# A transformer block on eight cores: the order of layer norm, key and value sums, and query filler

## The chip, the cores and the metric

One Trainium2 chip, eight cores, one launch. Each core writes its own rows of the output. The metric is the device time in microseconds of the slowest core. TensorE multiplies, VectorE (DVE) and ScalarE (ACT) take results out of PSUM and do the element work, GpSimd (POOL) masks and issues the DMAs of weights, SyncE (SP) issues the other loads.

## The reference, cut to what matters

```python
q = (x @ Wq).reshape(B, T, H, Dh)      # x already normalised; 4 x 4096 x 2048, 16 heads
k = (x @ Wk).reshape(B, T, H, Dh)
v = (x @ Wv).reshape(B, T, H, Dh)
scores = jnp.einsum('bthd,bshd->bhts', q, k)
scores = scores * jnp.tril(jnp.ones((T, T)))      # masked scores are 0, not minus infinity
attn = jax.nn.softmax(scores / T ** 0.5, axis=-1)
out = jnp.einsum('bhts,bshd->bthd', attn, v).reshape(B, T, H * Dh)
return out @ Wo
...
x = x + _layernorm(attention(_layernorm(x)))
x = x + _layernorm(ffn(_layernorm(x)))            # ffn: silu(g * gs) * (u * us), then down, 5632 wide
```

Since a masked score is 0, every masked key still counts with weight exp(0) = 1. For a query tile, all key tiles behind it contribute the plain sum of their rows of V.

## The kernel before

Two cores share one batch of 4096 rows, in 32 tiles of 128. The **even core** (side 0) owns tiles 0 to 17, the **odd core** (side 1) tiles 18 to 31. Keys and values are needed for all tiles up to the last own one: 18 on the even core, 32 on the odd one. The even core's other 14 tiles (`sd.tail`) are never keys; only the sum of their normalised rows is used.

**Phase A** (`phase_a`). Work is recorded in program order for each engine, with semaphores between; nothing is reordered afterwards. `stats(t)` loads a tile of x and takes its mean and variance (DVE, then Ln and Exp on ACT), `apply(t)` normalises it (DVE, into `xn`), `turn(t, hf)` transposes half of it on TensorE and copies it out on ACT. `ln_steps` hands out such steps between the projection tiles. `proj_unit` computes V or K for a chunk of up to four tiles and one group g of 512 columns (four heads), with the weights in `wres[0]` (V) or `wres[1]` (K). A tile is 16 matmuls of 512 columns; ACT and DVE copy the tiles out by turns into `stg`, and a unit is stored to DRAM. The program order is V and K of group 0 chunk by chunk, then V1, K1, V2, K2, V3, K3.

`vsum` adds the rows of each V tile: one matmul of the staged tile with a 64-column window of `ebig`, which has ones in columns 31 and 63, so that the sum of tile u lands in rows u and 32+u of bank 6. `vsum_out(g)` copies these sums to `vs`. On the even core it also adds the tail: `tail_sum` needs all 14 tail tiles summed in `xsum` on DVE, splits that sum in two bf16 parts, turns it by 32 matmuls of one column into `sbig`, and 32 matmuls `ps<-wres,sbig` bring it through the weights of V. In group 0 this stands right behind V0.

**Phase B** (`phase_b`) runs heads one after the other, and in a head blocks of up to four query tiles. A step s is 1024 columns of scores: `qk(s)` on TensorE, `exp(s)` on ACT (with a causal mask on POOL), two steps later `pv(s - 2)`, and sums of the weights on DVE (`zacc`) or TensorE (`zmm`). `pv` of a block's first step begins with the product of `ind` and `vs` (the skipped tiles' sums), and waits for `mul` of the block two before, which frees its bank. Projection Q of the next head is filler: single matmuls that a credit rule puts behind the work of a step, from step `q_from` of a head on. The even core has 25 steps in a head. Phase W is the output projection with its layer norms, phase C the ffn.

The helpers record everything, so the trace shows `mm` as L326, transposes as L331, DVE copies as L348, DVE tensor_tensor as L349, ACT copies as L359 and ACT activations as L360.

Of the kernel before, what the change touches and what calls it, by code (L numbers as in the profile page):

```python
# [7 lines left out]
BF16 = mybir.dt.bfloat16  # L8
# [18 lines left out]
class Side:  # L27

    def __init__(self, k):  # L30
        self.k = k
        if k == 0:
            self.own = list(range(NA))
            self.order = list(range(NT))
            self.blocks = [(4, 4), (8, 4), (12, 4), (16, 2), (0, 4)]
            self.npe = {4: 1, 8: 2, 12: 2, 16: 2, 0: 0}

            self.lag = {4: 2, 8: 2, 12: 1, 16: 0, 0: 2}
            self.ffn = [4, 4, 4, 3, 3]
            self.npt = 6  # L40
            self.q_from = 12
        else:
            self.own = list(range(NA, NT))
            self.order = self.own + list(range(NA))
            self.blocks = [(18, 4), (22, 4), (26, 4), (30, 2)]
            self.npe = {18: 2, 22: 3, 26: 3, 30: 2}
            self.lag = {18: 3, 22: 3, 26: 3, 30: 3}
            self.ffn = [4, 4, 3, 3]
            self.npt = 7

            self.q_from = 30
        self.keys = list(range(self.own[-1] + 1))
# [65 lines left out]
def build_nc():  # L118
# [43 lines left out]
    sh.onesb = small("onesb", [128, 128], BF16)  # L162
    sh.ebig = small("ebig", [128, 96], BF16)
    sh.c64 = small("c64", [64, 128], BF16)
# [235 lines left out]
def phase_a(c):  # L400
# [102 lines left out]
    pend = []  # L503

    def flush_vsum():
        while pend:
            pend.pop(0)()

    def proj_tile(kind, g, cc, i, slot, who):
# [23 lines left out]
        if kind == "k":  # L533
            ev = evac(c, who, c.stg[slot][:, i * W:(i + 1) * W], bank(c, pb)[:, 0:W], w)
        else:
            sv = c.stg[slot][:, 0:4 * W].rearrange("p (h t) -> p h t", h=4)[:, :, i * 128:(i + 1) * 128]
            ev = evac(c, who, sv, bank(c, pb).rearrange("p (h t) -> p h t", h=4), w)
            u = gt + i
            first = cc == 0 and i == 0
            fin = cc == len(sd.chunks) - 1 and i == nt - 1 and not sd.tail  # L540

            def vsum(u=u, sv=sv, ev=ev, slot=slot, first=first, fin=fin):
                w = [ev, ev_const] + ([c.ev_vs] if first else [])
                ev_vsmm[slot] = mm(c, bank(c, 6)[0:64, :], c.ebig[:, 31 - u:95 - u], sv, start=first,
                                   stop=fin, waits=w, inc=True)
            pend.append(vsum)
        ev_pb[pb] = ev
        return ev

    hh = {"n": 0, "idx": 0}  # L550

    n_step = 2 * n_key + len(sd.tail)
    rate = 1.0 if not sd.tail else 1.6

# [11 lines left out]
    def proj_unit(kind, g, cc):  # L566
        slot = ct["unit"] % (2 if g == 0 else 4)
        ct["unit"] += 1
# [4 lines left out]
        for i in range(nt if kind == "v" else 4):  # L573
            if g == 0:
                need = 2 * (p0 + (i + 1 if kind == "v" else nt))
                ln_steps(need if hh["idx"] < 4 else max(need, int(hh["idx"] * rate) + 6))
                hh["idx"] += 1
            who = "act" if i % 2 == 0 else "dve"
            evs.append(proj_tile(kind, g, cc, i, slot, who))
# [6 lines left out]

    def tail_sum():
# [4 lines left out]
        e2 = vop(c, "tt", c.xlo[:], c.xsum[:], c.xhi[:], ALU.subtract, waits=[e1])  # L592
        o = bank(c, 7)
        for j in range(ND):
            f = slice(j * 128, (j + 1) * 128)
            mm(c, o[:, j:j + 1], c.xhi[:, f], c.onesb[:, 0:1], start=True, stop=False,
               waits=[e2, ev_const] if j == 0 else ())
# [5 lines left out]
        c.ev_lump_w = e  # L603

    def vsum_out(g):

        flush_vsum()
        if sd.tail:
            if g == 0:
                tail_sum()  # L610
            for k in range(32):
                j = k % 16
                mm(c, bank(c, 6)[0:64, :], c.sbig[:, k * 64:(k + 1) * 64],
                   c.wres[0][:, j * 512:(j + 1) * 512], start=False, stop=(k == 31),
                   waits=[c.ev_lump] if k == 0 else (), inc=(k == 31))
        e = r.mark("pe")
        cols = slice(g * 512, (g + 1) * 512)
        e1 = vop(c, "copy", c.vs[:, cols], bank(c, 6)[0:64, :], waits=[e])
        c.ev_vs = vop(c, "tt", c.vs[32:64, cols], bank(c, 6)[32:64, :], c.vs[32:64, cols],
                      ALU.subtract, waits=[e1])  # L620
    c.ev_vs = None

    def turn_next(H_):

        t, hf = H_ // 2, H_ % 2
        if t < 4:

            if hf == 0 and t > 0:
                stats(t)
                apply(t)  # L630
            turn(t, hf)
            if H_ == 7:
                stats(4)
                apply(4)
                stats(5)
# [7 lines left out]
    for cc in range(nch):  # L643
        proj_unit("v", 0, cc)
        if cc < nch - 2:
            proj_unit("k", 0, cc)
    vsum_out(0)
    for g in range(1, 4):
        ev_w[f"v{g}"] = dma(c, "gpsimd", "qw0", c.wres[0][:], d["wv"].ap()[g], waits=[r.mark("pe")])
        for cc in range(nch - 2 if g == 1 else 0, nch):  # L650
            if g > 1 and cc % 2 == 1:
                next_cast(c, [r.mark("pe")])
            proj_unit("k", g - 1, cc)
        if g == 1:
# [3 lines left out]
        ev_w[f"k{g}"] = dma(c, "gpsimd", "qw1", c.wres[1][:], d["wk"].ap()[g], waits=[r.mark("pe")])  # L658
        for cc in range(nch):
            if cc % 2 == 1:  # L660
                next_cast(c, [r.mark("pe")])
            proj_unit("v", g, cc)
        vsum_out(g)
# [38 lines left out]
def phase_b(c):  # L702
# [71 lines left out]
    fill = q_ops(0)  # L774
    for _ in range(ND):
        fill.pop(0)[0]()
    flush_q()

# [12 lines left out]
    ev_lnread = {}  # L791
    end_step = {}
    for s, (bi, h, n, k, u, last) in enumerate(steps):
        if last:
            end_step[bi] = s
    nb = len(blocks)
    all_pe = [t0 == 0 for t0, nt in sd.blocks]

    at_sum, at_ln, at_mul = {}, {}, {}
    for b in range(nb):  # L800
        late = sd.lag[sd.blocks[blocks[b][1]][0]]
        if not all_pe[blocks[b][1]]:
            at_sum.setdefault(end_step[b] + 2 + late, []).append(b)
        at_ln.setdefault(end_step[b] + 3 + late, []).append(b)
        at_mul.setdefault(end_step[b] + 4 + late, []).append(b)

# [133 lines left out]

    zlag = 4

# [6 lines left out]
    for s in range(N):  # L949
        first_step.setdefault((steps[s][1], steps[s][2]), s)  # L950
    fs = {"credit": 0.0, "next": (0, 1), "free": 0}

    def pop_fill(s):
        f, cost, first, last = fill.pop(0)
        f()
        if last:
            fs["free"] = s + 2
# [4 lines left out]
    for s in range(N + 8):  # L962
        if s < N:
# [8 lines left out]
        work = passes(s) if s < N else 0  # L972
        if 2 <= s < N + 2:
            pv(s - 2)
            work += passes(s - 2)
            if by_pe(s - 2) and not all_pe[steps[s - 2][2]]:
                zmm(s - 2)
                work += passes(s - 2)
        if zlag <= s < N + zlag and all_pe[steps[s - zlag][2]]:
            zmm(s - zlag)  # L980
            work += passes(s - zlag)
# [4 lines left out]
        fs["credit"] = min(fs["credit"] + mean - work, 4.0)  # L986
        while fill and ((fs["credit"] > 0 and (not fill[0][2] or s >= fs["free"]))
# [477 lines left out]
```

How the kernel before makes its waits and increments, by code:

```python
                def emit(E, items):  # L212
                    for it in items:
                        if it[0] == "w":
                            E.wait_ge(sems[it[1]], it[2])
                        else:
                            inst = it[1](E)
                            if it[2] is not None:
                                inst.then_inc(sems[it[2]], it[3])
```

## Time and profile before

| | us |
|---|---|
| median of 3 runs | 3820.43 |
| the runs | 3819.45, 3820.43, 4373.15 |
| the profiled execution | 3820.14 |
| its span on the slowest core (core 0, even) | 3818.6 |
| spans of the even cores 0, 2, 4, 6 | 3818.6, 3815.7, 3810.7, 3815.8 |
| spans of the odd cores 1, 3, 5, 7 | 3806.7, 3801.6, 3810.4, 3801.4 |

The span runs from the first to the last instruction of a core; the execution's own time is 1.5 us longer than the longest span. Even and odd cores run different programs, and the time is that of whichever kind ends last. In the trace an engine's idle time is put down to the event that came last before it went on. A matmul's shape stands as rows*columns of the weights, then rows x columns of the moving data.

### The profile page before, as it was taken

How to read it: one execution, taken by the hardware profiler on the slowest of the kernel's cores; microseconds unless marked ns; L12 is line 12 of the kernel's file. 1: busy time of each engine (PE TensorE's matmuls, PEld its weight loads, DVE VectorE, ACT ScalarE, POOL GpSimd, SP SyncE). 2: the span in 40 equal slices, each digit the busy share in tenths (PEclk: the TensorE clock that was granted, in tenths of full speed). 3: DMA queues.
4: the chain of work that ended last, by engine and by line, in shares of the span. 5: the costliest groups of instructions: out<-in, count | busy, mean ns of one | idle time of the engine just before them, and what ended most of it. 6: DMA issues, size and time to landing. Idle time of an engine off the chain costs nothing.

```text
span 3818.6 us, 46783 instructions; the slowest of 8 cores (3801.4 to 3818.6 us)
## 1 busy us (share of the span) xinstructions
PE 3609.5 (95%) x18312; PEld 1749.5 (46%) x18312; DVE 1098.2 (29%) x1661; ACT 810.1 (21%) x1196; POOL 227.0 (6%) x290
## 2 busy tenths in 40 slices
PE   5779999988888888998999999999999999999998
PEld 2334444444444444444444444444444456645653
DVE  4841011455555554662111120102111121111112
ACT  2310000466666563332100011000011001101100
POOL 0000000111111110000000020000200001002000
PEclk8989999999999999999999999999999999999999
DMA  6556786488877306656445554453745548666664
GB/s 178 195 130 126 121 136 109 78 124 123 143 141 136 79 19 188 203 178 232 154 158 194 155 191 166 180 185 111 241 155 182 176 141 276 235 211 213 226 207 174
DMA packets 144657, 627.17 MB, mean 164 GB/s; under 512 B 47152, under 2 KB 75952, under 8 KB 114864
## 3 DMA queue, kind: packets, MB, share of 16 engines
q1 hardware_dynamic: 69744, 442.53, 34.4%
q0 software_dynamic: 13168, 134.22, 20.0%
q10 hardware_dynamic: 61520, 47.33, 4.1%
q8 instruction: 152, 2.49, 0.3%
q14 instruction: 73, 0.60, 0.1%
HBM read 660.74 MB, written 143.65 MB: 211 GB/s over the span
## 4 chain that ended last, share of the span: by engine, by line
PE 87%; DMA 3%; DVE 3%; ACT 3%; issue 2%; POOL 0%; ACTq 0%; SPq 0%; DVEq 0%; POOLq 0%
PE ps L326 86%; ACT pt L360 2%; DMA dp<-dwc 1%; DVE bna L352 1%; DVE zad L349 1%; PE ps L331 1%; DMA wo_sb<-woc 1%; DMA wres<-wv 1%; DMA xst<-x 1%; DMA yscr<-xy 1%; POOL pt L355 0%; ACT rz L360 0%; DVE xsum L351 0%; DVE aall L349 0%; ACT xown L359 0%
## 5 line engine op out<-in xcount | busy, mean ns | idle before, releaser
L326 PE MATMUL ps<-zt,slab 128*128 128x512 bf16 (+1 forms) x7040 | 1371.9, 358 | 9.8 <-DVE xy L351 8.1
L326 PEld LDWEIGHTS ps<-zt,slab 128*128 128x128 bf16 x7040 | 689.1, 98 | 691.4 <-issue 12.3
L326 PE MATMUL ps<-dp,hall 128*128 128x512 bf16 x3036 | 656.7, 379 | 1.1 <-DMA dp<-dwc 1.1
L351 DVE SCALAR_TENSOR_TENSOR hall<-ps,us_sb,sg 128x512 bf16<-128x512 f32 (+1 forms) x220 | 153.4, 697 | 1154.4 <-PE ps L326 1146.7
L326 PEld LDWEIGHTS ps<-dp,hall 128*128 128x128 bf16 x3036 | 296.7, 98 | 360.0 <-issue 3.0
L360 ACT ACTIVATE sg<-ps,gs_sb 128x512 f32<-128x512 f32 (+1 forms) x220 | 140.9, 645 | 1118.8 <-PE ps L326 1118.7
L360 ACT ACTIVATE pt<-ps 128x1024 bf16<-128x1024 f32 (+2 forms) x400 | 345.9, 895 | 95.1 <-PE ps L326 82.3
L326 PE MATMUL ps<-wres,xown 128*128 128x512 bf16 x1152 | 274.0, 394 | 13.4 <-DMA wres<-wv 8.4
L326 PE MATMUL ps<-xown,wqh 128*128 128x512 bf16 (+1 forms) x1280 | 273.9, 358 | 0.0
L326 PE MATMUL ps<-wo_sb,aall 128*128 128x512 bf16 x1152 | 256.1, 384 | 11.3 <-DMA wo_sb<-woc 11.3
L326 PE MATMUL ps<-xown,wres 128*128 128x512 bf16 (+1 forms) x1280 | 253.5, 360 | 0.0
L326 PE MATMUL ps<-qh,kh 128*128 128x512 bf16 (+3 forms) x928 | 214.0, 324 | 32.3 <-ACT pt L360 29.3
L349 DVE TENSOR_TENSOR zad<-zad,pt 128x1024 f32<-128x1024 f32 (+4 forms) x304 | 195.5, 673 | 98.1 <-ACT pt L360 44.8
L349 DVE TENSOR_TENSOR fall<-ps,dsb_sb 128x512 f32<-128x512 f32 x72 | 45.1, 684 | 598.8 <-PE ps L326 598.8
L326 PE MATMUL ps<-pt,vh 128*128 128x512 bf16 (+3 forms) x928 | 214.5, 324 | 0.0
L326 PEld LDWEIGHTS ps<-wres,xown 128*128 128x128 bf16 x1152 | 110.9, 100 | 157.5 <-issue 45.4
L326 PEld LDWEIGHTS ps<-xown,wres 128*128 128x128 bf16 x1280 | 125.0, 98 | 125.0 <-issue 4.9
L326 PEld LDWEIGHTS ps<-wo_sb,aall 128*128 128x128 bf16 x1152 | 112.9, 99 | 147.2 <-issue 18.9
L326 PEld LDWEIGHTS ps<-xown,wqh 128*128 128x128 bf16 x1280 | 123.9, 98 | 123.0
L360 ACT ACT_TABLE_LOAD x11 | 14.1, 1283 | 757.4 <-DVE mv L353 746.5
L349 POOL TENSOR_TENSOR fall<-fall,yl 128x1024 f32<-128x1024 f32 x30 | 74.1, 2470 | 1685.7 <-DVE fall L350 1483.6
L348 DVE CAST stg<-ps 128x512 bf16<-128x512 f32 (+1 forms) x76 | 50.4, 663 | 407.1 <-PE ps L326 407.1
(94 smaller groups left out, 1738.2 us busy)
## 6 DMA issues: line engine op xcount, KB each, us to landing
slab<-gwc SPq DMA_DIRECT2D x55, 2048.0 KB, 8.7
slab<-uwc SPq DMA_DIRECT2D x55, 2048.0 KB, 8.4
dp<-dwc SPq DMA_DIRECT2D x209, 512.0 KB, 3.9
xst<-x SPq DMA_DIRECT2D x32, 1024.0 KB, 5.6
gwc<-gw POOLq DMA_DIRECT2D x11, 2048.0 KB, 18.2
uwc<-uw POOLq DMA_DIRECT2D x11, 2048.0 KB, 34.1
dwc<-dw POOLq DMA_DIRECT2D x8, 2816.0 KB, 30.1
xy<-x SPq DMA_DIRECT2D x18, 1024.0 KB, 5.2
```

Source lines behind the costliest of these rows:

```text
L326: return c.r.op("tensor", lambda E: E.matmul(out, lhsT, rhs, start=start, stop=stop), waits=waits, inc="pe" if inc else None)
L331: return c.r.op("tensor", lambda E: E.transpose(out, in_, c.idn[:]), waits=waits, inc="pe" if inc else None)
L348: "copy": lambda E, o, i: E.tensor_copy(o, i),
L349: "tt": lambda E, o, a, b, op: E.tensor_tensor(o, a, b, op),
L351: "stt": lambda E, o, a, s, b, op0, op1: E.scalar_tensor_tensor(o, a, s, b, op0, op1),
L352: "bn": lambda E, o, i: E.bn_stats(o, i),
L360: "act": lambda E, o, i, f, **kw: E.activation(o, i, f, **kw),
```

## The change

- `turn_next`: in the first four tiles, `stats(t + 1)` and `apply(t + 1)` stand right behind the second half of tile t's transposes, instead of ahead of the first half of tile t + 1's. Both sides.
- `vsum`: only of tiles that some own query skips (`skips`: 13 of 32 on the odd core, 17 of 18 on the even one). On the odd core the window of `ebig` is 128 columns wide instead of 64.
- Even core only: the pace of layer norm steps (`pace`) is 1.3 steps a tile up to the last key tile and 0.6 behind it, so that the tail runs on into V1; the tail's sum is turned before V1's last chunk, V0's share is kept open in bank 7 and finished before K3's last two chunks, for which the weights V0 are loaded once more.
- Both sides: the loads of the first Q weights and two casts come behind V1.
- Even core only in effect: `pv` of a block's first step is held back until `o_gap` = 2 steps behind the `mul` it needs; Q filler starts at step 6 of a head instead of 12, with two blocks of Q ahead of the first head, a larger credit and one step instead of two between filler blocks.

```diff
     def turn_next(H_):
...
         if t < 4:
 
-            if hf == 0 and t > 0:
-                stats(t)
-                apply(t)
             turn(t, hf)
+            if hf == 1:
+                stats(t + 1)
+                apply(t + 1)
             if H_ == 7:
-                stats(4)
-                apply(4)
                 stats(5)
             return
...
+    skips = [gt + i for own, t0, gt, nt in sd.chunks for i in range(nt) if gt + i > sd.own[0]]
+    vbank = [7 if sd.tail else 6, 6, 6, 6]
...
-            first = cc == 0 and i == 0
-            fin = cc == len(sd.chunks) - 1 and i == nt - 1 and not sd.tail
+            first, fin = u == skips[0], u == skips[-1] and not sd.tail
+            m = 64 if sd.tail else 128
...
-                ev_vsmm[slot] = mm(c, bank(c, 6)[0:64, :], c.ebig[:, 31 - u:95 - u], sv, start=first,
+                ev_vsmm[slot] = mm(c, bank(c, vbank[g])[0:m, :], c.ebig[:, 31 - u:31 - u + m], sv, start=first,
                                    stop=fin, waits=w, inc=True)
-            pend.append(vsum)
+            if u in skips:
+                pend.append(vsum)
...
-    rate = 1.0 if not sd.tail else 1.6
+
+    def pace(idx):
+
+        if not sd.tail:
+            return idx + 6
+        n = int(1.3 * idx) + 6
+        return n if n <= 2 * n_key else 2 * n_key + int(0.6 * (idx - (2 * n_key - 6) / 1.3))
...
-    vsum_out(0)
+    flush_vsum()
+    if not sd.tail:
+        vsum_out(0)
...
+            if sd.tail and g == 1 and cc == nch - 2:
+                tail_parts()
+            if sd.tail and g == 1 and cc == nch - 1:
+                tail_sum()
...
+    if sd.tail:
+        ev_w["v0"] = dma(c, "gpsimd", "qw0", c.wres[0][:], d["wv"].ap()[0], waits=[c.ev_v3])
...
+        if sd.tail and cc == nch - 2:
+            vsum_out(0)
         proj_unit("k", 3, cc)
...
+        p = max(s + 2, pv_step[-1] if s else 0)
+        if k == 0 and bi >= 2:
+            p = max(p, mul_step[bi - 2] + sd.o_gap)
+        if len(pv_at.get(p, ())) == 2:
+            p += 1
```

ACT of the odd core, from the start of its own program (the copies are tile 0's transposes, `lva` and `rsa` its Ln and Exp, the cast V's first tile). Before:

```order
L359 COPY xown_147<-ps 128x8x128 x2
L359 CAST stg_1_148<-ps 128x4x128
L360 ACTIVATE lva_57<-mva_55,eps 128x1
L360 ACTIVATE rsa_59<-lva_57 128x1
L359 COPY xown_147<-ps 128x8x128 x2
```

and changed:

```order
L368 COPY xown_147<-ps 128x8x128 x2
L369 ACTIVATE lva_57<-mva_55,eps 128x1
L369 ACTIVATE rsa_59<-lva_57 128x1
L368 CAST stg_1_148<-ps 128x4x128
L368 COPY xown_147<-ps 128x8x128 x2
```

Tile 1's Ln and Exp moved ahead of the cast that waits for V's first tile.

TensorE of the odd core in V1, where the own tiles (`xown`) end and the others (`xoth`) begin. Before:

```order
L326 MATMUL ps<-wres_76,xown_147 128x512 x16
L326 MATMUL ps<-stg_1_149,ebig 64x512
L326 MATMUL ps<-wres_76,xoth_146 128x512 x16
L326 MATMUL ps<-stg_1_149,ebig 64x512
L326 MATMUL ps<-wres_76,xoth_146 128x512 x16
L326 MATMUL ps<-stg_1_150,ebig 64x512
```

and changed:

```order
L335 MATMUL ps<-wres_76,xown_147 128x512 x16
L335 MATMUL ps<-stg_1_149,ebig 128x512
L335 MATMUL ps<-wres_76,xoth_146 128x512 x16
L335 MATMUL ps<-stg_1_149,ebig 128x512
L335 MATMUL ps<-wres_76,xoth_146 128x512 x272
L335 MATMUL ps<-xown_147,wres_77 128x512 x192
```

The sums that stay are 128 columns wide, and behind the last of them 17 tiles of V (272 matmuls) and then K1 follow without one.

TensorE of the even core, the last block of one head and the first of the next (`qh,kh` scores, `pt,vh` PV, `xown,wqh` Q filler). Before:

```order
L326 MATMUL ps<-qh_0_112,kh_0_96 128x512 x2
L326 MATMUL ps<-ind_sb,vs 128x512
L326 MATMUL ps<-pt_0_102,vh_0_97 128x512
L326 MATMUL ps<-pt_0_102,vh_0_97 128x384
L326 MATMUL ps<-xown_85,wqh_0_110 128x512 x16
L326 MATMUL ps<-qh_0_112,kh_0_96 128x512
L326 MATMUL ps<-qh_0_112,kh_0_96 128x384
L326 MATMUL ps<-pt_0_103,vh_0_97 128x256
L326 MATMUL ps<-pt_0_103,vh_0_97 128x128
L326 MATMUL ps<-qh_0_112,kh_0_96 128x256
L326 MATMUL ps<-qh_0_112,kh_0_96 128x128
L326 MATMUL ps<-ind_sb,vs 128x512
```

and changed:

```order
L335 MATMUL ps<-qh_0_112,kh_0_96 128x512 x2
L335 MATMUL ps<-ind_sb,vs 128x512
L335 MATMUL ps<-pt_0_102,vh_0_97 128x512
L335 MATMUL ps<-pt_0_102,vh_0_97 128x384
L335 MATMUL ps<-xown_85,wqh_0_110 128x512 x4
L335 MATMUL ps<-qh_0_112,kh_0_96 128x512
L335 MATMUL ps<-qh_0_112,kh_0_96 128x384
L335 MATMUL ps<-pt_0_103,vh_0_97 128x256
L335 MATMUL ps<-pt_0_103,vh_0_97 128x128
L335 MATMUL ps<-xown_85,wqh_0_110 128x512 x4
L335 MATMUL ps<-qh_0_112,kh_0_96 128x256
L335 MATMUL ps<-qh_0_112,kh_0_96 128x128
```

The block of 16 Q matmuls is spread over the steps, and the next block's `ind_sb,vs` comes a step later.

## Rows read from the trace of the kernel before

**Rows 1.** Cores: span in us, mean granted TensorE clock.

```profile
core 0: 3818.6 us, clock 0.986
...
core 5: 3810.4 us, clock 0.994
```

**Rows 2.** Core 5 by stage, busy us (instructions), then PEclk, DMA share, GB/s.

```profile
core 5: us, PE busy (x) PEld busy (x) DVE busy (x) ACT busy (x) POOL busy (x), PEclk, DMA share, GB/s
0.00:80.00 80.00, 38.18 (x181) 18.51 (x182) 31.02 (x51) 17.20 (x31) 2.02 (x12) 0.85 0.70 172
...
1032.00:1990.00 958.00, 947.68 (x5151) 487.69 (x5152) 850.88 (x978) 804.23 (x943) 78.79 (x136) 1.00 0.35 80
```

**Rows 3.** Core 5, start, timeline: start, us, engine, operation, idle before.

```profile
27.41 2.47 DVE L352 BATCH_NORM_STATS2 bna<-xst 128x6 f32<-128x512 f32 x4 [8.56 <-issue]
...
27.80 5.92 PE L326 MATMUL ps<-wres,xown 128*128 128x512 bf16 x16 [6.93 <-DMA wres<-wv]
...
31.85 0.53 POOL L322 DMA_DIRECT2D wres<-wk  x1 [28.90 <-DMA xst<-x]
...
33.92 0.58 ACT L359 CAST stg<-ps 128x512 bf16<-128x512 f32 x1 [9.62 <-PE ps L326]
34.41 0.30 ACT L360 ACTIVATE lva<-mva,eps 128x1 f32<-128x1 f32 x1
...
36.60 1.86 PE L331 MATMUL ps<-idn,xn 128*128 128x128 bf16 x16 [2.88 <-DVE xn L350]
...
39.78 5.06 PE L326 MATMUL ps<-wres,xown 128*128 128x512 bf16 x16 [1.31 <-ACT xown L359]
...
73.18 3.62 PE L326 MATMUL ps<-xown,wres 128*128 128x512 bf16 x16
```

**Rows 4.** Core 5, DMA issues of the start, median us to landing.

```profile
wres<-wk POOLq DMA_DIRECT2D x1, 2048.0 KB, 17.6
```

**Rows 5.** Core 5, V's second column group, timeline.

```profile
345.64 3.63 PE L326 MATMUL ps<-wres,xown 128*128 128x512 bf16 x16
...
349.20 0.11 PEld L326 LDWEIGHTS ps<-stg,ebig 128*64 128x64 bf16 x1 [0.42 <-issue]
349.20 0.40 PE L326 MATMUL ps<-stg,ebig 128*64 128x512 bf16 x1
...
349.54 2.76 PE L326 MATMUL ps<-wres,xown 128*128 128x512 bf16 x12
```

**Rows 6.** Core 5, groups by form: count, busy, mean ns, idle before.

```profile
L326 PE MATMUL ps<-stg,ebig 128*64 128x512 bf16 x128 | 51.5, 403 | 3.8 <-DVE stg L348 3.8
```

**Rows 7.** Core 0, chain that ended last: start, us, what (pieces).

```profile
1057.43 11.63 PE ps L326 x63
...
1105.04 11.63 PE ps L326 x63
...
1769.10 773.83 PE ps L326 x3584
```

**Rows 8.** Core 0 by stage, columns as in Rows 2.

```profile
150.00:255.00 105.00, 60.78 (x257) 24.95 (x256) 74.39 (x113) 11.62 (x32) 1.59 (x3) 0.77 0.38 128
...
698.00:1448.00 750.00, 675.96 (x3653) 337.85 (x3654) 436.06 (x648) 455.40 (x630) 109.05 (x178) 1.00 0.61 103
```

**Rows 9.** Core 0, end of V's first group, TensorE timeline.

```profile
171.33 3.61 PE L326 MATMUL ps<-wres,xown 128*128 128x512 bf16 x16 [0.67 <-DVE stg L348]
198.90 0.61 PE L326 MATMUL ps<-stg,ebig 128*64 128x512 bf16 x1 [23.96 <-ACT stg L359]
...
242.47 9.98 PE L326 MATMUL ps<-wres,sbig 128*64 128x512 bf16 x32 [1.16 <-DVE sbig L348]
```

**Rows 10.** Core 0, same stretch, DVE, one tail tile's sum.

```profile
185.35 2.35 DVE L351 SCALAR_TENSOR_TENSOR xsum<-xst,rsa,xsum 128x2048 f32<-128x2048 f32 x1
```

**Rows 11.** Core 0, TensorE waits in attention: us in total, times, longest.

```profile
PE ps L326 <- DVE aall L349: 35.9, 30, 1.5
PE ps L326 <- ACT pt L360: 28.3, 61, 0.8
```

More of the change, by code:

```diff
@@ L40, in __init__ @@
             self.npt = 6
-            self.q_from = 12
+            self.q_from = 6
+            self.q_gap = 1
+            self.q_pre = 2
+            self.q_cap = 8.0
+            self.o_gap = 2
         else:
@@ L51, in __init__ @@
             self.q_from = 30
+            self.q_gap = 2
+            self.q_pre = 1
+            self.q_cap = 4.0
+            self.o_gap = 0
         self.keys = list(range(self.own[-1] + 1))
@@ L162, in build_nc @@
     sh.onesb = small("onesb", [128, 128], BF16)
-    sh.ebig = small("ebig", [128, 96], BF16)
+    sh.ebig = small("ebig", [128, 160], BF16)
     sh.c64 = small("c64", [64, 128], BF16)
@@ L566, in proj_unit @@
     def proj_unit(kind, g, cc):
-        slot = ct["unit"] % (2 if g == 0 else 4)
+        slot = ct["unit"] % (4 if hh["n"] == n_step else 2)
         ct["unit"] += 1
@@ L591, in tail_sum @@
         e1 = vop(c, "copy", c.xhi[:], c.xsum[:], waits=[e])
-        e2 = vop(c, "tt", c.xlo[:], c.xsum[:], c.xhi[:], ALU.subtract, waits=[e1])
-        o = bank(c, 7)
+        c.ev_xparts = vop(c, "tt", c.xlo[:], c.xsum[:], c.xhi[:], ALU.subtract, waits=[e1])
+    def tail_sum():
+        o = bank(c, 4)
         for j in range(ND):
@@ L602, in tail_sum, with lump @@
         c.ev_lump = vop(c, "copy", B[:, NA + 32, :], B[:, NA, :], waits=[e])
-        c.ev_lump_w = e
+    def lump(g):
+        for k in range(32):
+            j = k % 16
+            mm(c, bank(c, vbank[g])[0:64, :], c.sbig[:, k * 64:(k + 1) * 64],
+               c.wres[0][:, j * 512:(j + 1) * 512], start=False, stop=(k == 31),
+               waits=[c.ev_lump, ev_w[f"v{g}"]] if k == 0 else (), inc=(k == 31))
     def vsum_out(g):
@@ L608, in vsum_out @@
         if sd.tail:
[L609 to L615, printed above, removed]
+            lump(g)
         e = r.mark("pe")
         cols = slice(g * 512, (g + 1) * 512)
-        e1 = vop(c, "copy", c.vs[:, cols], bank(c, 6)[0:64, :], waits=[e])
-        c.ev_vs = vop(c, "tt", c.vs[32:64, cols], bank(c, 6)[32:64, :], c.vs[32:64, cols],
+        ob = bank(c, vbank[g])
+        e1 = vop(c, "copy", c.vs[:, cols], ob[0:64, :], waits=[e])
+        c.ev_vs = vop(c, "tt", c.vs[32:64, cols], ob[32:64, :], c.vs[32:64, cols],
                       ALU.subtract, waits=[e1])
@@ L653, in phase_a @@
             proj_unit("k", g - 1, cc)
+        ev_w[f"k{g}"] = dma(c, "gpsimd", "qw1", c.wres[1][:], d["wk"].ap()[g], waits=[r.mark("pe")])
+        for cc in range(nch):
+            if g > 1 and cc % 2 == 1:
+                next_cast(c, [r.mark("pe")])
+            if sd.tail and g == 1 and cc == nch - 2:
+                tail_parts()
+            if sd.tail and g == 1 and cc == nch - 1:
+                tail_sum()
+            proj_unit("v", g, cc)
+        vsum_out(g)
         if g == 1:
@@ L657, in phase_a @@
                         for h in range(2)]
[L658 to L663, printed above, removed]
+            next_cast(c, [r.mark("pe")])
+            next_cast(c, [r.mark("pe")])
         c.ev_v3 = r.mark("pe")
+    if sd.tail:
+        ev_w["v0"] = dma(c, "gpsimd", "qw0", c.wres[0][:], d["wv"].ap()[0], waits=[c.ev_v3])
     for cc in range(nch):
@@ L774, in phase_b @@
     fill = q_ops(0)
-    for _ in range(ND):
-        fill.pop(0)[0]()
-    flush_q()
+    for _ in range(sd.q_pre):
+        for _ in range(ND):
+            fill.pop(0)[0]()
+        flush_q()
     blocks = [(h, n) for h in range(H) for n in range(len(sd.blocks))]
@@ L791, in phase_b @@
     ev_lnread = {}
[L792 to L795, printed above, removed]
     nb = len(blocks)
     all_pe = [t0 == 0 for t0, nt in sd.blocks]
+    pv_step, pv_at, mul_step = [], {}, {}
     at_sum, at_ln, at_mul = {}, {}, {}
[L800 to L805, printed above, removed]
+    for s, (bi, h, n, k, u, last) in enumerate(steps):
+        p = max(s + 2, pv_step[-1] if s else 0)
[3 more added lines that the diff above has]
+            p += 1
+        pv_step.append(p)
+        pv_at.setdefault(p, []).append(s)
+        assert s < NPT or pv_step[s - NPT] <= s
+        if last:
+            late = sd.lag[sd.blocks[n][0]]
+            if not all_pe[n]:
+                at_sum.setdefault(p + late, []).append(bi)
+            at_ln.setdefault(p + 1 + late, []).append(bi)
+            at_mul.setdefault(p + 2 + late, []).append(bi)
+            mul_step[bi] = p + 2 + late
     def S(s):
@@ L939, in mul @@
                          ALU.mult, waits=[ev_rz[bi], ev_last_pv[bi], c.ev_a_pe])
-    zlag = 4
+    z_at = {}
+    for s in range(N):
+        if all_pe[steps[s][2]]:
+            z_at.setdefault(pv_step[s] + 2, []).append(s)
     def passes(s):
@@ L950, in phase_b @@
         first_step.setdefault((steps[s][1], steps[s][2]), s)
-    fs = {"credit": 0.0, "next": (0, 1), "free": 0}
+    fs = {"credit": 0.0, "next": (0, sd.q_pre), "free": 0}
     def pop_fill(s):
@@ L960, in pop_fill @@
         return cost
-    for s in range(N + 8):
+    for s in range(N + 12):
         if s < N:
@@ L972, in phase_b @@
         work = passes(s) if s < N else 0
[L973 to L981, printed above, removed]
+        for p in pv_at.get(s, ()):
+            pv(p)
+            work += passes(p)
+            if by_pe(p) and not all_pe[steps[p][2]]:
+                zmm(p)
+                work += passes(p)
+        for p in z_at.get(s, ()):
+            zmm(p)
+            work += passes(p)
         for b in at_sum.get(s, ()):
@@ L985, in phase_b @@
             load_kv(h + 1)
-        fs["credit"] = min(fs["credit"] + mean - work, 4.0)
+        fs["credit"] = min(fs["credit"] + mean - work, sd.q_cap)
         while fill and ((fs["credit"] > 0 and (not fill[0][2] or s >= fs["free"]))
```

14 lines of the change are left out of this document (7 added, 7 removed).

## The prediction

> **What bounds the kernel now.** I read the spans of the cores first. The longest is an even core's, 3818.6 us, and the profiled execution took 3820.14, so 1.5 us lie around the span. The longest odd core ends only 8.2 us earlier, at 3810.4 [rows 1]. Whatever the even core gains beyond some 8 us shows only as far as the odd core gains too. So I make two sums, and the larger is the forecast.
>
> Then the stages. On the odd core TensorE is busy 948 of 958 us in attention, at a granted clock of 1.00; there is nothing to win there but instructions. The start is different: 38 of the first 80 us busy, at 0.85, so partly at the lower of its two levels [rows 2]. On the even core there are two more holes: 61 busy of the 105 us around the end of V0, at 0.77, and 676 of 750 in attention [rows 8]. A matmul of 512 columns costs TensorE 773.83 / 3584 = 0.216 us when nothing waits [rows 7]; that is the unit for all that follows.
>
> **The odd core, part by part.**
>
> *Sums of V that go.* In V1 one tile and its sum take 349.54 - 345.64 = 3.90 us [rows 5]. Sixteen matmuls are 3.45 (3.46 unrounded), so a sum costs 0.44, twice its 0.216. There are 128 now [rows 6], 32 in each group; 13 in each stay, so 76 go: 76 x 0.44 = **33.4 us**. TensorE is the bound behind the first 80 us, so all of it is on the path; the copies of V tiles by ACT and DVE (0.58 for one on ACT [rows 3]) take turns and hide under 3.45 a tile.
>
> *Sums that stay, widened.* The extra 0.22 us shows in the rows as the weight load: a 64-column load starts only with its matmul, with 0.42 us idle ahead of it, where loads usually run ahead [rows 5]. By that rule the 52 sums would come down to 0.216, without it they could stay at 0.44; the trace shows the gap but not its cause. From the rows alone the bounds are 0 and 52 x 0.22 = 11.4 us. I take **11.4**, because the 3584 matmuls of [rows 7], all 128 columns wide, keep the spacing of 0.216 though the data differ.
>
> *The last sum of a group.* TensorE waits four times, 3.8 us in total, for the DVE copy of the last tile [rows 6]. The last tile is one that no query skips, so this goes: **3.8 us**.
>
> *The start.* V0 runs from 27.80 to 33.7. Tile 1's statistics begin at 27.41 and last some 2.8 us, so they are there at 30.3, but its Ln stands behind the cast of V0's tile on ACT and runs at 34.41; the transposes come at 36.60 and V's second tile at 39.78 [rows 3]. With Ln and Exp ahead of the cast, `xn` is ready at 30.3 + 0.7 + 1.3 = 32.3, before V0 ends. The transposes start at 33.7 and the second tile, 3.2 us behind them as now, at 36.9. From then on the next tile's transposes follow at once: 3.2 for transposes and copies plus one V tile. K's first tile starts at 73.18 now [rows 3]. With V tiles as slow as now (5.1 to 5.9 us) the third starts at 45.6, the fourth at 54, K at 60; with tiles at the full clock from the third on (3.6, as K's first [rows 3]) K starts at 56. DVE needs about 5.4 us for statistics, normalising and cast of a tile, less than the 7 to 9 of a tile on TensorE. K's weights are issued at 31.85 and land 17.6 us later [rows 3, 4], at 49.5, early enough. So K starts 13 to 17 us earlier; I take **15**. The lower bound is that other waits move in, as tiles of x, each 1 MB, are asked for faster: 3 us, the gain of tile 1 alone.
>
> *Moved DMAs.* The loads of the first Q weights and two casts move behind V1 on POOL's queue. The Q weights are not needed until K3 is over, hundreds of us later, and the two casts that the odd core no longer issues in V1 are made up in attention, where its DMA share is 0.35 [rows 2]. Cost zero under that cover; without it the first head would wait for a load of half the size of K's weights, so under 18 us [rows 4]. The wider `ebig` is one larger memset on POOL while it waits for nothing. Attention on the odd core keeps its order: its filler numbers are the old ones and `o_gap` is 0.
>
> Sum for the odd core: 3810.4 + 1.5 - 33.4 - 11.4 - 3.8 - 15 = **3748.3 us**.
>
> **The even core, part by part.** The same start, 15 us; four sums go, 2 us. At the end of V0, TensorE goes idle 23.96 us for a copy on ACT that is stuck behind the tail's layer norm, and the granted clock is 0.77 over the stretch [rows 8, 9]. From 171.33 until the 32 matmuls of `sbig` end at 252.4 it does work of five V tiles, six sums, 32 narrow matmuls and those 32, which at full speed is 17.3 + 2.6 + 0.8 + 7.3 = 28 us of 81 [rows 9]. So 53 us go if the tail hides. It now has 0.6 tail tile for each projection tile. A tail tile costs DVE 2.5 us for statistics [rows 3] and 2.35 for the sum [rows 10], 5.5 with the small steps between, so 0.6 x 5.5 + 0.35 for the cast is 3.65 us against 3.45 (K) to 3.9 (V) on TensorE. That is nearly even; up to 5 us may come back as waits. I take 50. The V0 weights are loaded again behind V3 and needed 12 tiles, 41 us, later; a load took 17.6 [rows 4].
>
> In attention a head takes 1105.04 - 1057.43 = 47.6 us [rows 7]. Its order holds 186.5 matmuls' worth of 512 columns (Q 72), 40.3 us. The waits are 35.9 us for `mul` and 28.3 for `exp` over 16 heads [rows 11]. Holding `pv` back two steps and putting Q filler into each step covers both in part. Bounds: nothing, or all 64; I take half, 32. The sum: 3820.1 - 15 - 2 - 50 - 32 = **3721 us**; without any gain in attention 3753. So the odd core sets the time, and the even core's reordering shows hardly at all.
>
> **The forecast** is 3748 us, 1.9% below the median of 3820.43, which is 0.3 us from the profiled execution. About 2% (3744.0) is what a measurement of this kernel can tell from no change.
>
> **Rivals.**
>
> *The wide sums cost what the narrow ones do.* For it: a sum's moving operand is a strided read of `stg`, and the rows do not separate that from the width. Against it: the V tile behind a sum pays too, whose operands are plain. The time is 3748 + 11.4 = 3760.
>
> *The start is bound by DMA.* Ahead of V's first tile TensorE waits 6.93 us for weights [rows 3], and x competes with 2 MB of K weights. If the later tiles then wait for x, only 3 of the 15 us come: 3760.
>
> *The even core stays last.* If holding PV back gains nothing and the tail on DVE costs 5 to 10 us, the even core ends at 3753 + 5 to 10 = 3758 to 3763.
>
> *Slower than before.* `pv` held back two steps keeps `pt` buffers (six on the even core) full; `exp` of step s needs the PV of step s - 6, and `qk` the `exp` of s - 2, so a late PV stops the score matmuls and then the heads' rhythm. It decides from a loss of (3820 - 3753) / 16 = 4.2 us a head, nearly one us at each of its five block starts; at 5 us a head the even core ends at 3833. For it: five block starts a head, and PVs that come in pairs. Against it: two steps of score work remain between the longest delay and that limit, and 7.3 us of slack in each head.
>
> *The start gains more.* If V's tiles run at the full level from the second on, K starts at 54, 19 us earlier, and the odd core ends at 3744; with odd cores as short as the best, it may be 3738.
>
> **How the numbers follow.** Forecast 0.64, wide sums 0.09, start bound by DMA 0.09, even core last 0.07, slower than before 0.02, more gain 0.09. The range takes in the three rivals above the forecast and most of the one below: 3739 to 3763. Faster by over 2% means under 3744.0: the last case and, of the forecast's own spread of about 5 us to either side, a third: 0.3. Slower by over 2% would be 3897, 9 us lost in each head: 0.01.
>
> **What would show it.** The odd core's span as the longest, near 3747, and core 0 some 20 to 50 us shorter. On the odd core: the first K matmul near 58 instead of 73; 52 sums of form 128*128 with spacing near 0.22; 17 V tiles in 58.7 us without a sum; attention as long as before. On the even core: no wait above a few us between 150 and 255, clock 1.00 there; a head near 45.5 us; few waits for `aall`. The prediction is wrong if the even core is last, if K still starts behind 65, or if DMA waits appear on the odd cores once both kinds enter the ffn at other times than now.

## The result, and the profile after

The changed kernel takes 3782.1 us (three runs, 3781.9, 3782.1 and 3785.3), the kernel before 3820.4 in the same session: a ratio of 0.990, 95% interval 0.988 to 0.9925. That is 38 us faster and 34 us above the forecast of 3748. Here and in the experiments a time is the median of the runs in which no die showed a lower granted clock, while the texts written ahead of the experiments go by medians over all runs (3783.7 here). The cores of the profiled execution (3785.3 us):

```profile
core 0: 3709.4 us, clock 0.992
...
core 5: 3779.7 us, clock 0.992
...
core 7: 3783.8 us, clock 0.991
```

The order of the two kinds is as forecast: an odd core is last, an even one 74 us ahead of it ([rows 1] had the even core last by 8). Core 0, with the 1.5 us that the execution takes beyond its longest span, came 10 us under the even core's forecast of 3721; the odd one missed 3747 by 37.

**The start.** Core 5, TensorE timeline, against [rows 3]:

```profile
34.91 3.61 PE L335 MATMUL ps<-wres,xown 128*128 128x512 bf16 x16 [1.72 <-ACT xown L368]
...
41.13 3.61 PE L335 MATMUL ps<-wres,xown 128*128 128x512 bf16 x16 [1.72 <-ACT xown L368]
...
58.08 5.08 PE L335 MATMUL ps<-xown,wres 128*128 128x512 bf16 x16
```

V's second tile starts at 34.91 instead of 39.78, K's first at 58.08 instead of 73.18. On cores 1, 3 and 7 K begins at 60.9, 59.5 and 58.6, some 11 to 13 earlier than before.

**The sums.** Core 7, TensorE timeline in V1, against [rows 5]:

```profile
307.77 3.62 PE L335 MATMUL ps<-wres,xown 128*128 128x512 bf16 x16
311.22 0.38 PE L335 MATMUL ps<-stg,ebig 128*128 128x512 bf16 x1
311.44 3.62 PE L335 MATMUL ps<-wres,xown 128*128 128x512 bf16 x16
```

A tile with its sum takes 311.44 - 307.77 = 3.67 us instead of 3.90, so a wide sum costs 0.22 instead of 0.44. The odd core's program now has 52.

**The stall.** So far the odd core follows the forecast. In K1, the stage behind V1, it then stands still. A cast, in what follows, is a DMA that POOL issues to rewrite a block of weights from f32 to bf16 in DRAM (`woc<-wo`, `gwc<-gw`, `uwc<-uw`). The kernel before has four of them inside V1 on the odd core; the change takes all four out, puts two behind V1 and leaves two to attention. K1 has four of its own in both. Core 7, timeline (all engines, some rows):

```profile
411.21 1.01 POOL L331 DMA_DIRECT2D woc<-wo  x2 [111.70 <-PE ps L335]
411.62 0.37 ACTq L331 DMA_DIRECT2D vscr<-stg  x1
412.21 0.54 POOL L331 DMA_DIRECT2D wres<-wv  x1
...
425.00 0.50 POOL L331 DMA_DIRECT2D woc<-wo  x1 [12.25 <-PE ps L335]
...
452.63 0.50 POOL L331 DMA_DIRECT2D woc<-wo  x1 [27.12 <-PE ps L335]
452.99 29.56 ACTq L331 DMA_DIRECT2D kscr<-stg  x1
488.47 0.65 ACT L368 CAST stg<-ps 128x256 bf16<-128x256 f32 x2 [39.14 <-DMA vscr<-stg]
488.99 11.26 PE L335 MATMUL ps<-xoth,wres 128*128 128x512 bf16 x44 [29.89 <-ACT stg L368]
```

Read it from below. TensorE waits 29.89 us for ACT's copy into `stg`; that copy waits for a store of V1, `vscr<-stg`, which was issued at 411.62 and so took until 488.4. `stg` has four buffers, and this one comes round again here. Cores 1, 3 and 5 wait 27.1, 23.0 and 30.3 us at the same place; before there is no wait. The landing times say the same. Core 7, DMA issues between 405 and 500 (median us to landing at the end of a row):

```profile
woc<-wo POOLq DMA_DIRECT2D x4, 2048.0 KB, 33.5
wres<-wv POOLq DMA_DIRECT2D x1, 2048.0 KB, 42.2
kscr<-stg ACTq DMA_DIRECT2D x3, 512.0 KB, 51.8
...
vscr<-stg ACTq DMA_DIRECT2D x1, 256.0 KB, 76.8
```

Before, the store of 256 KB at this place lands in 2.3 us and the K stores in 18.1 (core 7, the same stage). Core 5 by stage, busy us, then clock, DMA share:

```profile
350.00:408.00 58.00, 58.00 (x270) 26.28 (x269) 5.61 (x9) 4.69 (x8) 0.00 (x0) 1.00 0.11 37
408.00:440.00 32.00, 32.00 (x150) 14.52 (x149) 4.65 (x7) 2.93 (x5) 2.05 (x4) 1.00 0.99 142
440.00:490.00 50.00, 19.70 (x116) 11.59 (x115) 2.14 (x4) 1.23 (x3) 0.50 (x1) 0.70 0.98 162
```

The DMA engines stand idle through V1, where the odd core now issues no casts (share 0.11; 0.73 before), and are full in K1 (0.98; 0.71 before). On the odd core the change added no bytes; it moved casts, and the load with them.

**The even core.** Core 0, chain that ended last, against [rows 7]:

```profile
1031.76 16.91 PE ps L335 x81
...
1075.42 16.91 PE ps L335 x81
```

and by stage, against [rows 8]:

```profile
698.00:1448.00 750.00, 726.44 (x3973) 366.12 (x3972) 469.38 (x709) 466.22 (x646) 108.96 (x173) 1.00 0.71 132
150.00:255.00 105.00, 86.95 (x405) 39.17 (x404) 71.80 (x111) 12.85 (x37) 2.12 (x4) 0.92 0.65 191
```

A head takes 43.66 us instead of 47.6: 63 us in 16 heads, all that the waits came to and not half. The 105 us around the end of V0 hold 87 of work instead of 61, with one wait of 12.3 us left, for a DVE copy; and 16.7 us of the store stall come to it too, at 372.

### The profile page after: what moved, and what is told of

It is laid out like the page before. It is cut to its first block, busy times and chain, and to the rows that moved or that the text cites. A ratio compares the mean times of both kernels' runs of the same rounds, so it can differ in the third digit from the quotient of the medians.

```text
span 3783.8 us, 50455 instructions; the slowest of 8 cores (3705.3 to 3783.8 us)
## 1 busy us (share of the span) xinstructions
PE 3685.2 (97%) x19252; PEld 1840.7 (49%) x19252; DVE 1424.9 (38%) x1860; ACT 1158.5 (31%) x1511; POOL 173.1 (5%) x235
## 4 chain that ended last, share of the span: by engine, by line
PE 94%; ACT 2%; DMA 1%; issue 1%; ACTq 1%; DVE 1%; another core or an unknown queue 0%; DVEq 0%; POOL 0%; POOLq 0%; SPq 0%
PE ps L335 93%; ACT pt L369 1%; PE ps L340 1%; ACTq L331 1%; DMA xst<-x 0%; DMA indf<-ind 0%; DVE bna L361 0%; DVE zad L358 0%; ACT rz L369 0%; DMA kscr<-stg 0%; ACT xy L369 0%; DVE xy L360 0%; ACT zst L368 0%; DVE xn L359 0%
## 5 line engine op out<-in xcount | busy, mean ns | idle before, releaser
L335 PE MATMUL ps<-zt,slab 128*128 128x512 bf16 (+1 forms) x5632 | 1069.0, 353 | 6.2 <-DVE xy L360 6.2
L369 ACT ACTIVATE pt<-ps 128x1024 bf16<-128x1024 f32 (+2 forms) x752 | 724.9, 981 | 132.9 <-PE ps L335 103.5
L358 DVE TENSOR_TENSOR zad<-zad,pt 128x1024 f32<-128x1024 f32 (+5 forms) x640 | 614.6, 975 | 59.5 <-POOL pt L364 2.9
L335 PE MATMUL ps<-dp,hall 128*128 128x512 bf16 x2332 | 504.0, 379 | 0.0
L335 PE MATMUL ps<-qh,kh 128*128 128x512 bf16 (+1 forms) x1760 | 432.4, 339 | 9.8 <-ACT qh L368 5.8
L335 PE MATMUL ps<-pt,vh 128*128 128x512 bf16 (+1 forms) x1760 | 432.3, 339 | 1.8 <-ACT pt L369 1.1
L335 PE MATMUL ps<-xoth,wres 128*128 128x512 bf16 (+1 forms) x1280 | 253.2, 359 | 29.9 <-ACT stg L368 29.9
L335 PE MATMUL ps<-wres,xoth 128*128 128x512 bf16 x1152 | 252.4, 379 | 0.0
L335 PEld LDWEIGHTS ps<-qh,kh 128*128 128x128 bf16 x1760 | 165.2, 98 | 176.8 <-issue 52.0
L335 PEld LDWEIGHTS ps<-pt,vh 128*128 128x128 bf16 x1760 | 165.6, 98 | 153.8 <-issue 14.1
```

The costliest lines, as they stand in the source:

```text
L335: return c.r.op("tensor", lambda E: E.matmul(out, lhsT, rhs, start=start, stop=stop), waits=waits, inc="pe" if inc else None)
L358: "tt": lambda E, o, a, b, op: E.tensor_tensor(o, a, b, op),
L369: "act": lambda E, o, i, f, **kw: E.activation(o, i, f, **kw),
```

## The experiments

**1. The suspected part undone.** The casts go back into V1, where the kernel before issued them, and the two behind V1 go; all else stays.

```
             for cc in range(nch):             # V of column group g
-                if g > 1 and cc % 2 == 1:
+                if cc % 2 == 1:
                     next_cast(c, [r.mark("pe")])
 ...
-                next_cast(c, [r.mark("pe")])      # behind V1
-                next_cast(c, [r.mark("pe")])
```

> The changed kernel with one edit undone: the casts stand inside V1 again, one behind every second chunk, and the two at once behind V1 are gone. In the changed kernel's trace two casts and the next load of V's weights are issued within 1.1 us, a store of 256 KB from V1 then takes 77 us to land, and TensorE waits 23 to 30 us in K1 on every odd core. Theory A (the burst of transfers on POOL's queue holds up the stores): the wait in K1 goes, the odd cores end 23 to 30 us earlier, at 3746 to 3756, and the time is about 3755. Rival B (the store is slow because the even cores are now in another stage and take the memory bandwidth): the wait stays within a few us or moves, and the time stays at 3780 to 3785.

Measured: 3745.7 us, 0.981 of before (0.979 to 0.983). Odd cores 3741 to 3744, even 3692 to 3695. Core 7's landing times in the stretch 405 to 500:

```profile
kscr<-stg ACTq DMA_DIRECT2D x6, 512.0 KB, 18.4
wres<-wv POOLq DMA_DIRECT2D x1, 2048.0 KB, 17.3
vscr<-stg ACTq DMA_DIRECT2D x1, 256.0 KB, 17.9
```

The wait for `stg` is gone on every odd core and the Q matmuls behind K3 start at 968.5 on core 5 instead of 998.9. So the moved casts cost the whole gap. This is the best version here, 36 us faster than the changed kernel (35 by the ratios to the kernel before, each in its own session).

**2. No casts at all in V1 or behind it.**

> The changed kernel without the two casts behind V1 and with none in V1 either; attention makes up for them, one at each head. Theory A: as with the casts back in V1, about 3755, since one cast at a time ahead of each load is harmless. If the loads of the Q weights or of V's weights by themselves are what hold the stores up, the wait in K1 stays at 20 us or more and the time above 3775.

Measured: 3746 and 3747 us in two runs, no stall. Where K1 is spared, it makes no difference whether V1 has casts.

**3. Four casts behind V1.**

```
+            next_cast(c, [r.mark("pe")])
+            next_cast(c, [r.mark("pe")])
```

> The changed kernel with four casts at once behind V1 instead of two. Each cast moves 4 MB in and 2 MB out, 20 us or so of the DMA engines. Theory A: the wait in K1 grows by about 40 us on the odd cores, to 60 to 70 us, and the time goes to about 3820. Rival B: no growth, or a few us; time 3785 to 3790.

Measured: one run, 3796; the stall is 37.3 to 40.4 us. It grew by 7 to 17 us a core, 11 on average, and not by 40, so bytes queued do not turn into waiting one for one. Why it stops there is shown below, behind experiment 6.

**4. The narrow sums, with the stall in place.** `m = 64`.

> The changed kernel with the sums of V on the odd core 64 columns wide again; their number stays at 13 in each group. If the width costs what the weight load's gap shows, the odd cores end 52 x 0.22 = 11.4 us later, at 3781 to 3795, and the time is about 3795. If width is nothing, the time stays at 3784. The stall in K1 depends on DMAs and stays.

Measured: 3788.5 (0.992; 0.990 to 0.994), 6.4 above the changed kernel. The stall is 23.4 to 26.4 us instead of 23 to 30.3. On core 7 V1 ends 4.0 us later, but the stall ends at 488.59 against 488.99, so the slower V1 only shortened the wait; on core 3 the stall ends 7.9 us later. The Q matmuls start 5.2, 5.8, 7.3 and 14.2 us later on cores 7, 5, 1 and 3. So with the stall in place the price cannot be read: part of it is hidden on some cores and not on others. Why the store lands sooner on core 7 (72.4 us instead of 76.8), though it and the casts are issued 4 us later, is not shown.

**5. The two casts singly, in K1's chunks 0 and 2, instead of together.**

```
-                if g > 1 and cc % 2 == 1:
+                if g > 1 and (cc % 2 == 1 or (g == 2 and cc in (0, 2))):
```

> The changed kernel with its two casts behind V1 moved to K1's first and third chunk, so that K1 has the same number of casts as in the changed kernel, but never two issued together. Theory A1 (what hurts is that several transfers are queued at once): the stall in K1 shrinks to under 10 us and the time is 3746 to 3760. Theory A2 (what hurts is the sum of what is moved in K1): the stall stays near 25 us on the odd cores and the time near 3780.

Measured: 3780.4 (0.990; 0.988 to 0.992), stall 27.6 to 31.4. Spacing them so does nothing; it is not the burst. The four casts of K1's first four chunks are issued 13 to 14 us apart on core 5, and one takes longer than that (19.7 us to land in the kernel before), so they still pile up.

**6. One cast behind V1 instead of two.**

> The changed kernel with one cast behind V1 instead of two, the other made up in attention. With two the stall was 30 us and with four 38 to 40. If each queued cast adds to the stall, one leaves 10 to 20 us of it, time 3758 to 3770; if a single one fits beside the stores as it does elsewhere in the phase, under 5 us, time 3746 to 3752.

Measured: 3749.6, 3750.6 and 3767.4 (0.984; 0.980 to 0.988). In the profiled run cores 1, 3 and 5 have no wait, core 7 has 6.1; the 256 KB store takes 46.0 us there. In the run of 3767.4 core 5 ends 24 us later than in the profiled one. Five casts in K1 are the edge, four (before, 1, 2) are safe, six stall.

**How a cast starves a store.** The queues' packets tell it. Core 7 of the changed kernel, DMA queues between 411 and 486, then between 485 and 500 (packets, MB, share of 16 engines; q0 carries what POOL issues, four casts and one load of weights here, q10 the stores):

```profile
q0 software_dynamic: 450, 10.49, 97.5%
q10 hardware_dynamic: 449, 0.23, 1.4%
...
q0 software_dynamic: 16, 0.00, 0.1%
q10 hardware_dynamic: 2208, 1.88, 36.7%
```

While both queues have work, they get one packet each in turn: 450 and 449 in 75 us. But a packet of q0 holds 10.49 / 450 = 23 KB on average and a store's 0.5, so the stores move 0.23 MB in 75 us, 6 packets a us. The moment the casts' queue is empty they move 2208 packets in 15 us, 147 a us, and the stall ends. Experiment 3 has the same, core 5 between 455 and 490, then core 7 from 410.3 to 494.5, the 84.2 us that V1's last store takes there:

```profile
q0 software_dynamic: 258, 5.31, 100.2%
q10 hardware_dynamic: 258, 0.13, 1.8%
...
q0 software_dynamic: 560, 13.11, 100.2%
q10 hardware_dynamic: 544, 0.28, 1.5%
```

The last two lines say why four casts cost only some 11 us more than two. The store lands at 494.5 while q0 still has work: its 0.28 MB went in 544 packets, all by turns, and once they have had their turns it is done, however much is queued beside it. In the changed kernel it had 449 packets through when q0 ran dry. So a store waits for as many turns as it has packets, or until the other queue is empty, whichever comes first.

The Trainium skill, DMA: Bandwidth & Descriptors, section Queues, rings and completion order, states this: each DMA engine "round-robins between the queue rows it has work for, at *packet* granularity". The trace of the changed kernel agrees to one packet in 450. In experiment 1 the casts' queue runs dry between casts, and stores pass there (core 5, 455 to 475):

```profile
q0 software_dynamic: 81, 2.13, 69.5%
q10 hardware_dynamic: 1056, 0.79, 12.0%
```

**7. The even core's change alone;** the odd core's program is as before.

> Only the even core's part of the change: the odd core's program is that of the kernel before, instruction for instruction on TensorE, the even core's that of the changed kernel. If the time is that of the kind that ends last, the even cores end near 3710 and the time is still 3809 to 3813, 0.2 to 0.3% below before. If the even cores' earlier end helps or hurts the odd ones through shared memory, the odd spans move by more than 5 us.

Measured: 3815.0 (1.000; 0.9986 to 1.001). The even cores end at 3728 to 3737, the odd at 3808 to 3813. Some 85 us gained on half of the cores show as nothing.

Two things came otherwise than expected. The odd spans did move by more than 5 us: they average some 3810 instead of 3803. A wait for `stg` of 3.9 to 5.3 us near 360 is new on cores 3, 5 and 7; whether the even cores' transfers cause it is open, since the odd core keeps one edit here, another use of the `stg` buffers around the end of V0. And the even cores end some 20 us later than 3710, with the program that they have in the changed kernel. There cores 0, 2 and 6 stall for 15.6 to 17.0 us in their K1 and core 4 for 4.9; here all four stall for 32.2 to 39.2, at the same place. Core 0 of the changed kernel, then of this run, DMA queues between 315 and 355:

```profile
q0 software_dynamic: 322, 6.88, 98.0%
...
q0 software_dynamic: 266, 5.14, 97.4%
```

The engines are as busy, but q0 moves 5.14 MB instead of 6.88. In this run the odd cores issue casts in V1, core 1 at 332.9, and in the changed kernel they do not. So how long a queue of casts lasts depends on what the other cores move as well.

**8. The casts as in 1, and the old order of the first tiles.**

```
+            if hf == 0 and t > 0:
+                stats(t)
+                apply(t)
             turn(t, hf)
-            if hf == 1:
-                stats(t + 1)
-                apply(t + 1)
```

> The kernel with the casts back in V1 (3745.8 us) and, of the change, the normalising ahead in the first four tiles undone on both sides. By the prediction the order of the start is worth 15 us: K's first tile starts near 73 instead of 58, and the time is 3761. If the transfers set the pace of the start, it is worth 3 us or less: 3749.

Measured: 3756.8 and 3757.0, 11 us above experiment 1. On core 5 K's first tile starts at 71.60 instead of 57.92, 13.7 later, but V1 at 306.32 instead of 296.57, only 9.8 later. Four us are given back right behind K's first tile: the next transposes wait 2.95 us for ACT's copy of the ones before, which in the order of ACT stands behind a later tile's Ln and Exp, and these wait for DVE's statistics; and the granted clock is 0.86. Core 5 of experiment 1 by stage:

```profile
58.00:68.00 10.00, 7.05 (x34) 2.97 (x32) 9.69 (x17) 4.19 (x10) 0.00 (x0) 0.86 0.66 225
```

With the old order the 10 us behind K's first tile hold 9.3 us of work at a clock of 1.00. DVE is busy for 9.69 of the 10 us shown: with tiles asked for faster, it is the limit there for a moment.

**9. Smaller packets.** The changed kernel, with each `woc` cast written as two halves of columns, so that the same bytes go in short runs.

```
-        todo.append((d["woc"].ap()[s, :], d["wo"].ap()[s, :]))
+        todo.append((d["woc"].ap()[s, :].rearrange("p (a b) -> a p b", a=2),
+                     d["wo"].ap()[s, :].rearrange("p (a b) -> a p b", a=2)))
```

> The changed kernel; only the casts of the output weights (woc) are written as two halves of columns, so that the same bytes go in runs of at most 4 KB read and 2 KB written instead of stretches of some tens of KB. Theory A (the small packets of K's and V's stores are served in turn with the casts' packets of 33 KB, and fall behind because of the packets' size): the stores keep their pace, the wait of ACT for stg in K1 falls from 23 to 30 us to under 10, and the time to 3750 to 3762. Rival B (only the bytes queued in K1 count): the wait stays 23 to 30 us on the odd cores and the time 3778 to 3790.

Measured: 3990 us, 1.048 of before (1.043 to 1.053). Neither theory had this. Core 5 between 455 and 485:

```profile
q0 software_dynamic: 328, 0.67, 11.8%
q10 hardware_dynamic: 1289, 1.01, 10.5%
```

The stall in K1 is gone on all odd cores and a K store lands in 10.8 us, as theory A says. But q0 now moves 0.67 MB in 30 us, a cast takes 90.3 us (core 7), and the weights queued behind them on POOL come late (core 5, waits):

```profile
PE ps L335 <- DMA wres<-wk: 126.5, 1, 126.5
PE ps L335 <- DMA wres<-wv: 88.1, 2, 81.4
```

A wait for `stg` of 18 to 22 us comes back in K3, where the casts are of the unsplit kind. The run confirms that a cast in flight is not by itself what holds a store up. It does not part packet size from the engines' load, since the share of the casts fell from 87.5% to 11.8% as well. The split was a poor cure.

**10. The move of the casts alone, on the kernel before.**

> The kernel before with one part of the change alone: the odd core's casts in V1 are taken out and the two of them stand behind V1, as in the changed kernel; sums, start and even core as before. Theory (moved casts starve the stores of K1): a wait of 20 to 30 us of ACT for stg appears in K1 of the odd cores, their spans grow to 3830 to 3840 and the time to 3835 to 3845. Rival (the stall needs the faster V1 or the earlier start): no wait over 5 us, 3818 to 3822.

Measured: 3838.8 (1.0058; 1.0036 to 1.0079), slower than before by 21 us. The edit stands in code that both kinds run, so, unlike what the text above says, the even core's two casts in V1 move as well; its spans stay at 3810 to 3817. Cores 5 and 7, waits in K1:

```profile
PE ps L326 <- ACT stg L359: 25.8, 1, 25.8
...
PE ps L326 <- ACT stg L359: 25.5, 1, 25.5
```

Cores 1 and 3 wait only 9.4 and 10.3 and end at 3817. The stall needs neither the faster V1 nor the new start.

**11. The narrow sums again, without the stall:** experiment 1 with `m = 64`.

> The version with the casts back in V1 (no stall in K1), with the odd core's sums 64 columns wide instead of 128. With the stall gone nothing can absorb the width. Theory (a change of width costs 0.22 us on each of 52 sums, as forecast): the odd cores' attention starts 11.4 us later, near 979 to 980, and the time is 3757. Rival (the width costs only half of that, as the 5.5 us measured with the stall would say): 3750 to 3752.

Measured: 3762.2 (0.985; 0.983 to 0.988), 16.5 above experiment 1. The Q matmuls start at 981.0, 978.0, 980.1 and 978.7 on cores 1, 3, 5 and 7, against 966.2, 970.2, 968.5 and 967.6: 11.3 later on average, as the theory has it, though single cores lie between 7.8 and 14.8. The other 5 us are lost behind it, at and behind the first score matmul. Core 5 of this run, then of experiment 1:

```profile
980.13 3.62 PE L335 MATMUL ps<-xown,wqh 128*128 128x512 bf16 x16
987.86 1.01 PE L335 MATMUL ps<-qh,kh 128*128 128x512 bf16 x2 [4.11 <-ACT qh L368]
```

```profile
968.50 3.62 PE L335 MATMUL ps<-xown,wqh 128*128 128x512 bf16 x16
973.37 0.59 PE L335 MATMUL ps<-qh,kh 128*128 128x512 bf16 x2 [1.25 <-ACT qh L368]
```

The score matmul comes 7.7 us behind the first Q tile instead of 4.9. By the profile ACT's copy of Q waits for a K store there, and the clock then falls (core 5 of this run by stage):

```profile
990.00:1000.00 10.00, 10.00 (x42) 4.22 (x41) 6.40 (x8) 5.76 (x8) 0.82 (x2) 0.83 0.00 0
```

**12. All 32 sums of each group, wide:** experiment 1 with the 76 sums back.

> The version with the casts back in V1, with all 32 sums of each group issued again on the odd core, but 128 columns wide; the 76 added ones are of tiles that no query skips. Theory (a wide sum costs the plain 0.216 us of a matmul of 512 columns, and nothing else hangs on it): 76 x 0.216 = 16.4 us, to which the wait for the last tile's copy returns, some 3 us: 3762 to 3766. Rival (a sum costs 0.44 whatever its width, the V tile behind it pays for the strided operand): 33 us, 3779.

Measured: 3771.9 (0.988; 0.986 to 0.991), 26 above experiment 1, between the two expectations. The Q matmuls start at 988.0, 987.8, 986.0 and 989.3 on cores 1, 3, 5 and 7, on average 19.7 later, and 76 x 0.216 + 3.8 is 20.2. The remaining 6 us come behind that; at the first head ACT's `qh` is waited for 2.4 to 5.9 us, against 1.3 in experiment 1.

## Why the prediction was wrong, step by step

**The failed step** is "*Moved DMAs*": "Cost zero under that cover". It cost 36 us, 3782.1 against 3745.7: a stall of 23.0 to 30.3 us in K1 and, behind it, a slower first head. I asked when the moved transfers were needed and what cover attention gave them. I did not ask what else would be in flight at their new place, though the stores of K1 run there through four `stg` buffers, nor what queue they would share engines with. The price given for lost cover, "under 18 us", was one load's landing time and for the wrong transfer: what came late was not the moved load but somebody else's store. The last line of the prediction named the symptom (DMA waits on odd cores) without a mechanism, at a wrong place, and gave it no chance, so the range did not hold it.

**Sums that go and stay, 33.4 + 11.4 + 3.8.** Right. Experiment 12 gives 19.7 for the 76 wide sums and the last waits, against 20.2. Experiment 11 gives 11.3 for the width of 52, against 11.4. The rival "wide sums cost what the narrow ones do" is out: 0.216 us is all that is left of one. Both agree with what the prediction cites from the Trainium skill, TensorEngine Tiling (Array Packing), section Tiling Modes, that changing the tiling mode drains TensorE; the runs show what the change of width costs, and not why.

**The start, 15.** Mechanism right, the term too large: 11 in the time (experiment 8). K began where I said, at 58.08 on core 5, but I counted the gain at K's first tile and stopped looking: behind it TensorE waits for ACT and DVE, and 4 us went back.

**Together.** For the odd core the terms gave 63.6 us. In experiment 1 core 5 is 1027.2 - 968.5 = 58.7 ahead at the first Q matmul, the start's 4 us short. Its whole span is 67 shorter. The 8 beyond are mostly that core's own: in the profiled run before it ends 4 to 9 us behind the other odd cores, and cores 3 and 7 shorten by 57 and 59 us, only 1 to 3 more than their lead. The longest odd core of the kernel before mostly ends near 3805, so the sum started from a span some 5 us too long, and that cancelled a start counted 4 us too large. That the version without the moved casts meets the forecast of 3748 so closely, at 3745.7, is partly luck.

**First head.** Not in the prediction: 8.0 us from first Q tile to first score on core 5 (5.0 before), plus a granted clock of 0.88 in the 10 us from 999; on core 3 it stays at 4.9. Experiments 11 and 12 also lose 5 to 6 us behind the first Q matmul. In the changed kernel the last cast of K3 lands in 24.1 us against 14.4 in experiment 1, and the K stores beside it in 19.0 against 10.1. Why these are slow in one and not the other stays open.

**The even core.** "50" for the tail was too much. At the first score matmul the changed kernel is 698.4 - 669.3 = 29 us ahead, where 67 were forecast for start, sums and tail; experiment 1 reaches 651.1, 47 ahead. So the tail gives some 30 and not 50, and of that the moved casts took 18, most of it the store stall. "Half of 64" in attention was too little: 63. Both errors lay on the core that does not set the time.

**The other rivals.** Start bound by DMA, even core last, PV held back: none came. Nor did the attention of the odd core change beyond its first head (busy 948.5 of 958 us on core 7).

## What to carry to other kernels

A DMA that is moved must be costed at its new place, by what else is in flight there and by which buffers those transfers free, and not by when its own data are needed. Where large casts and small stores share the engines, count how long the queue of casts stays non-empty, and how many packets a store has: it advances by one packet for each of theirs, and four buffers last only so long. And an edit on a compute engine ahead of a wait for DMA cannot be priced there, since the wait takes up a part of it on some cores (experiment 4: 6 us, against 16 in experiment 11); price it where the wait is gone.

## What the runs showed of the hardware

- Two DMA queues with work take turns by packets, whatever their size: 450 to 449, 258 to 258, 560 to 544. A store of 256 KB took 76.8 us beside casts, 2.3 without.
- Issuing a store stopped ACT for 29.56 us, where it takes 0.37, while earlier stores stood behind casts; the traces do not show what it waited for.
- With the 16 engines 97 to 98% busy, a core's queue of casts and loads moved 6.88 MB in 40 us while the odd cores issued no casts, and 5.14 MB while they did.
- Casts in short runs moved 0.67 MB in 30 us with the 16 engines busy only 11.8% of the time; what limited them is not shown.
- A matmul of 64 columns between matmuls of 128 costs 0.22 us (11.3 / 52) more than one of 128.
